# A graph network's edge phase: shifted tables, scans from PSUM, wide casts, and a later scatter

## The reference

```python
def conv(x, W_l, b, W_r):
    agg = segment_sum(x[src], dst, N); deg = segment_sum(1, dst, N)
    return (agg / max(deg, 1)) @ W_l + b + x @ W_r
h = relu(conv(x, W1_l, b1, W1_r))
h = relu(conv(h, W2_l, b2, W2_r))
out = layernorm(x + h @ W3 + b3)      # all float32, biases not zero
```

## Time and profile before

| | |
|---|---|
| median of 3 runs | 3070.76 us (3068.34 to 3070.82) |
| profiled execution | 3069.83 us, span 3068.0 us |
| busy in the span | PE 2858.7, DVE 2459.7, ACT 2066.8, POOL 2239.5 us |
| granted TensorE clock, mean | 0.974 |
| DMA | 488.23 MB, 159 GB/s |

### The profile page before, as it was taken

One profiled execution on the slowest core, in us unless ns is written; L12 is line 12 of the kernel. 1 busy time (PEld: TensorE's weight loads), 2 busy tenths in 40 slices (PEclk: granted clock), 3 DMA queues, 4 the chain that ended last, 5 costly groups with the idle time before them and its releaser, 6 DMA issues. The chain is left out here.

```text
span 3068.0 us, 56367 instructions
## 1 busy us (share of the span) xinstructions
PE 2858.7 (93%) x18433; PEld 2560.7 (83%) x18433; DVE 2459.7 (80%) x4095; ACT 2066.8 (67%) x3188; POOL 2239.5 (73%) x1830
## 2 busy tenths in 40 slices
PE   5999999999999999999999999999998887887885
PEld 4898888888888888888888888888888776777775
DVE  5888888888887878878888788787887876777775
ACT  3777677676766777767767676677776655555554
POOL 5777777777777777777777777777776677777776
PEclk9999999999999999999999999999999898989898
DMA  3444444444444445444444444444443655555553
GB/s 128 147 164 152 156 153 155 150 158 157 157 156 147 161 145 164 151 157 151 155 152 159 156 157 155 146 163 145 164 151 128 211 192 174 193 181 188 194 175 118
DMA packets 253118, 488.23 MB, mean 159 GB/s; under 512 B 37615, under 2 KB 165206, under 8 KB 253090
## 3 DMA queue, kind: packets, MB, share of 16 engines
q1 hardware_dynamic: 202498, 387.58, 37.4%
q0 software_dynamic: 50176, 99.91, 10.8%
q10 hardware_dynamic: 416, 0.40, 0.0%
HBM read 284.67 MB, written 206.22 MB: 160 GB/s over the span
## 5 line engine op out<-in xcount | busy, mean ns | idle before, releaser
L494 ACT ACTIVATE h_full<-pair,bias 128x512 f32<-128x512 f32 x784 | 531.5, 684 | 632.0 <-PE pair L866 616.9
L655 DVE TENSOR_TENSOR h_lo<-h_full,h_hi 128x1024 fp32r<-128x1024 f32 x392 | 658.0, 1679 | 174.7 <-ACT h_hi L496 174.7
L390 POOL TENSOR_TENSOR xb<-xn,b_row 128x1024 f32<-128x1024 f32 x196 | 470.7, 2402 | 225.7 <-DVE y L671 223.8
L344 POOL DMA_INDIRECT xe<-in_x_dram,e_stage x392 | 500.7, 1277 | 177.0 <-issue 97.7
L877 PE MATMUL pair<-w_hi,h_hi 128*128 128x256 f32 x1960 | 553.2, 282 | 30.4 <-DVE h_lo L655 28.7
L877 PE MATMUL pair<-w_hi,h_lo 128*128 128x256 f32 x1960 | 543.0, 277 | 0.0
L877 PE MATMUL pair<-w_lo,h_hi 128*128 128x256 f32 x1960 | 542.5, 277 | 0.0
L856 PE MATMUL pair<-ident,xn 128*128 128x128 f32 x2352 | 336.4, 295 | 128.7 <-DMA xn<-h_tab,c_stage 119.4
L856 PEld LDWEIGHTS pair<-ident,xn 128*128 128x128 f32 x2352 | 301.6, 154 | 163.7 <-issue 115.1
L496 ACT CAST h_hi<-h_full 128x1024 fp32r<-128x1024 f32 x392 | 412.7, 1053 | 12.5
L877 PEld LDWEIGHTS pair<-w_hi,h_hi 128*128 128x128 f32 x1960 | 367.8, 188 | 55.4 <-DVE h_lo L655 51.8
(11 more groups left out here) (117 smaller groups left out, 6583.8 us busy)
## 6 DMA issues: line engine op xcount, KB each, us to landing
xn<-in_x_dram SPq DMA_DIRECT2D x196, 512.0 KB, 3.9
out_dram<-o SPq DMA_DIRECT2D x196, 512.0 KB, 2.7
seg<-seg_tab SPq DMA_DIRECT2D x74, 512.0 KB, 5.0
xdb_tab<-xdb SPq DMA_DIRECT2D x49, 512.0 KB, 4.7
h_tab<-src_h SPq DMA_DIRECT2D x49, 512.0 KB
h_tab<-dst_h SPq DMA_DIRECT2D x49, 512.0 KB, 6.2
xn<-h_tab SPq DMA_DIRECT2D x49, 512.0 KB, 5.2
xb<-xdb_tab SPq DMA_DIRECT2D x49, 512.0 KB, 4.1
```

What stands on the lines that cost most here:

```text
L344: nc.gpsimd.indirect_dma_start(out=xe[:, kind, s], out_offset=None, in_=x, in_offset=bass.IndirectOffsetOnAxis(ap=e_stage[:, kind, s:s + 1 ...
L390: nc.gpsimd.tensor_tensor(xb[:, b], xn[:, u], b3_row[:, :].unsqueeze(1).to_broadcast([P, S, D]), ALU.add).then_inc(xb_ok, 1)
L494: nc.scalar.activation(h_full[:, n, k], ps[:, k], ACT.Relu, bias=bias[:, n, k:k + 1]).then_inc(hf_ok[n], 1)
L655: nc.vector.tensor_tensor(h_lo[:, h], h_full[:, n], h_hi[:, h].bitcast(f32), ALU.subtract).then_inc(hlo_ok[n], 1)
```

## The change

The tables now hold max(z, -b1) instead of z+b1. Since relu(z+b1) = max(z,-b1)+b1, and the segment mean of a constant over a destination's sources is the constant, the readers use the shifted value and b1 moves into the second layer's bias: b2 + W2_r'b1 + W2_l'b1. PE computes the two products once, between the stages (24 matmuls of two columns), from `b1_hi` and `b1_lo`, which DVE makes at the start; DVE adds b2 (`bias_c`). With no relu left to take, the scans read `pair[0]` in PSUM directly, ACT's relu into `h_full` is gone, and `xe_hi`, `xe_lo`, `h_hi`, `h_lo` are each made by one 1024-wide instruction. DVE's step begins with the residual of j-2 and takes its statistics between the means and `mean_low`; ACT's step finishes tile j-3 ahead of `second`, and takes the deviation of j-2 at its end; POOL's step scatters tile j-4. PE's transpose into `pair[0]` waits for the scans of the tile before. The end of the phase drains one tile more.

```diff
             def step(j, b, left):                                   # POOL
                 if left > 1:
                     fetch(j + 2, b)
-                if not (isinstance(j, int) and j < 3):
-                    scatter(j - 3, 1 - b)
+                if not (isinstance(j, int) and j < 4):
+                    scatter(j - 4, b)
                 if not left:
...
+                    for n in range(j - 3, j + 1):
+                        scatter(n, n % 2)
...
-            def front(j, b):                                        # ACT
...
+            def dst_high(j, b):
+                act.wait_ge(c_hd_ps, (j + 1) * K)
+                nc.scalar.copy(xe_hi[:, b], pair[1][:, :, :]).then_inc(c_hdhi_ok, 1)
...
+            def second(j, k):
+                after(act, c_hlo_ok, j)
                 act.wait_ge(c_l2_ps, j * K + k + 1)
+                nc.scalar.activation(h_full[:, 1, k], pair[2][:, k], ACT.Relu, bias=bias_c[:, k:k + 1]).then_inc(c_hf_ok, 1)
+            def second_high(j, b):
+                act.wait_ge(c_hf_ok, (j + 1) * K)
+                nc.scalar.copy(h_hi[:, b], h_full[:, 1]).then_inc(c_hhi_ok, 1)
...
             def step(j, b, left):
                 if left:
-                    front(j + 1, 1 - b)
-                if not (isinstance(j, int) and j < 2):
-                    deviation_edges(j - 2, b)
-                second(j, b, 0)
-                if left:
-                    mean_high(j + 1, 1 - b)
-                second(j, b, 1)
+                    dst_high(j + 1, 1 - b)
                 if isinstance(j, int) and j == 0:
                     for n in range(2):
                         act.wait_ge(y_out[n], 16 * (NG // 2))
+                if not (isinstance(j, int) and j < 3):
+                    finish_edges(j - 3, 1 - b)
+                second(j, 0)
+                if left:
+                    mean_high(j + 1, 1 - b)
+                second(j, 1)
+                second_high(j, b)
                 if not (isinstance(j, int) and j < 2):
+                    deviation_edges(j - 2, b)
+                if not left:
                     finish_edges(j - 2, b)
...
             low_h(0, 0, 0)                                          # DVE, start
+            dve.wait_ge(b_in, 96)
+            nc.vector.tensor_scalar(b1_row[:, :], b1_row[:, :], -1.0, None, ALU.mult).then_inc(b1_ok, 1)
+            nc.vector.tensor_copy(b1_hi[:, :, :], bias[:, 0].unsqueeze(2).to_broadcast([P, K, 2])).then_inc(b1_ok, 1)
+            dve.wait_ge(b1_ok, 2)
+            nc.vector.tensor_tensor(b1_lo[:, :, :], ..., b1_hi[:, :, :].bitcast(f32), ALU.subtract).then_inc(b1_ok, 1)
...
-                                            b1_row[:, :].unsqueeze(1).to_broadcast([P, S, D]), ALU.add).then_inc(src_ok, 1)
+                                            b1_row[:, :].unsqueeze(1).to_broadcast([P, S, D]), ALU.max).then_inc(src_ok, 1)
...
+            def scan(j, b):                                         # DVE, edge phase
+                dve.wait_ge(c_seg_in[b], slot_use(j, b))
+                for k in range(K):
+                    dve.wait_ge(c_hs_ps, j * K + k + 1)
+                    dve.wait_ge(c_run_ok, j * K + k + 1)
+                    nc.vector.tensor_tensor_scan(run[:, k], seg_of(b)[:, 0:G], pair[0][:, k], run[:, k, G - 1:G], ALU.mult, ALU.add)\
+                        .then_inc(c_run_ok, 1)
...
+            def low_dst(j, b):
+                dve.wait_ge(c_hdhi_ok, j + 1)
+                nc.vector.tensor_tensor(xe_lo[:, b], pair[1][:, :, :], xe_hi[:, b].bitcast(f32), ALU.subtract).then_inc(c_hdlo_ok, 1)
...
+            def low_second(j, b):
+                dve.wait_ge(c_hhi_ok, j + 1)
+                nc.vector.tensor_tensor(h_lo[:, b], h_full[:, 1], h_hi[:, b].bitcast(f32), ALU.subtract).then_inc(c_hlo_ok, 1)
...
             def step(j, b, left):
                 early = isinstance(j, int) and j < 2
                 if not early:
+                    residual_edges(j - 2, b)
+                if not (isinstance(j, int) and j < 3):
+                    factors_edges(j - 3, 1 - b)
                 if left:
+                    scan(j + 1, 1 - b)
+                    low_dst(j + 1, 1 - b)
+                    means(j + 1, 1 - b)
                 if not early:
+                    sums(j - 2, b, c_y_ok, c_stats_ok)
                 if left:
                     mean_low(j + 1, 1 - b)
+                if not early:
+                    averages_edges(j - 2, b)
+                low_second(j, b)
...
+            pe.wait_ge(y_ok, NG - 1)                                # PE, between the stages
+            pe.wait_ge(b1_ok, 3)
+            for m in range(K):
+                first = True
+                for w in (X2R, X2L):
+                    for k in range(K):
+                        for wx, a in ((w_hi, b1_hi), (w_lo, b1_hi), (w_hi, b1_lo)):
+                            ins = nc.tensor.matmul(pair[2][:, 0, 2 * m:2 * m + 2], wx[:, w, k, m * P:(m + 1) * P], a[:, k],
+                                                   start=first, stop=w == X2L and k == K - 1 and a is b1_lo)
+                            first = False
...
             def turn_edges(j, b):
                 pe.wait_ge(c_hs_in[b], slot_use(j, b, 16 * S))
-                after(pe, c_hs_ok, j * K)
+                pe.wait_ge(c_run_ok, (j + 1) * K)
```

More of the change, by code:

```diff
@@ L811, in factors_edges @@
                 factors(j, b, c_sd_ok, c_rs_ok, c_nb_ok)
-            for k in range(K):
-                scan(0, 0, k)
+            scan(0, 0)
+            low_dst(0, 0)
             means(0, 0)
-            for k in range(K):
-                low_dst(0, 0, k)
+            dve.wait_ge(bias_ps, 1)
+            nc.vector.tensor_tensor(bias_c[:, :], pair[2][:, 0, 0:2 * K].rearrange("p (k a) -> p k a", a=2)[:, :, 0], bias[:, 1],
+                                    ALU.add).then_inc(bias_ok, 1)
             mean_low(0, 0)
+            dve.wait_ge(o_ok, NG)
             def step(j, b, left):
@@ L822, in step @@
                 if not early:
-                    dve.wait_ge(c_stats_ok, j - 1)
+                    residual_edges(j - 2, b)
+                if not (isinstance(j, int) and j < 3):
+                    factors_edges(j - 3, 1 - b)
                 if left:
-                    scan(j + 1, 1 - b, 0)
+                    scan(j + 1, 1 - b)
+                    low_dst(j + 1, 1 - b)
+                    means(j + 1, 1 - b)
                 if not early:
[L827 to L834, removed]
-                    factors_edges(j - 2, b)
+                    sums(j - 2, b, c_y_ok, c_stats_ok)
                 if left:
                     mean_low(j + 1, 1 - b)
-                low_second(j, b, 1)
-                if isinstance(j, int) and j == 0:
-                    dve.wait_ge(o_ok, NG)
-                else:
-                    residual_edges(j - 1, 1 - b)
-                if not left:
-                    averages_edges(j - 1, 1 - b)
-                    factors_edges(j - 1, 1 - b)
-                    residual_edges(j, b)
-                    averages_edges(j, b)
-                    factors_edges(j, b)
+                if not early:
+                    averages_edges(j - 2, b)
+                low_second(j, b)
+                if not left:
+                    factors_edges(j - 2, b)
+                    for n, c in ((j - 1, 1 - b), (j, b)):
+                        residual_edges(n, c)
+                        sums(n, c, c_y_ok, c_stats_ok)
+                        averages_edges(n, c)
+                        factors_edges(n, c)
             edge_passes(dve, step)
```

54 lines of the change are left out of this document (16 added, 38 removed).

## The result

The changed kernel took 3079.2 us (median of 7 runs, 3074.89 to 3083.91) against 3069.92 for the kernel before (7 runs on the same chip, 3067.49 to 3073.29): a ratio of 1.003, 95% interval 1.0018 to 1.0042. It is slower by 0.3%; 3042 had been forecast. Its profiled execution took 3074.89 for a span of 3073.1.

The account below looks back on a forecast made before the run. POOL, issuing eight indirect DMAs and two small copies a step, was taken to bound the edge phase. Steps -25.6, head -7.0, tail +3.8 and start +0.6 summed to -28.2: median 3042 from 3070.76, own range 3021 to 3055, whole range 3008 to 3063.

Parts of the forecast that it names:

- The change does its work in the second: Of two stages, row tiles up to about 2380 and then the edge phase, the edge phase was to hold the gain.
- Rival B: Edge phase: the two buffers of `o` and the scatter's landing become the loop, step 14.3, 3084; chance 0.11.
- the step: One edge tile's round on POOL, between fetch ends: 13.91 to 13.3 over 42 steps, -25.6.
- The bare time of 12.0: Edge phase: a step with no POOL issue or copy stretched by DVE; stretching is the time beyond it, 1.9 before.
- the squares: Edge phase: stretching of POOL goes with summed squares of DVE hold lengths, 7.16 to 4.47; stretching 1.2, step 13.2.
- a placement: Edge phase: DVE holds laid by hand against POOL's issues; stretching 1.55 with landing at F+9, F a fetch's end, 0.9 at F+11.
- Residual first, wide casts: Edge phase: the new DVE order and 1024-wide operations stay off POOL's path; DVE's 10.5 a step loses some 0.3.
- ACT's order is the risk: Edge phase: ACT's `second` stands behind the wait for the scatter's landing; PE's `mean_low` was still to be in time.
- Head and tail: Ends of the edge phase, scatter four behind: -7.0 until the end of fetch 6, +3.8 after fetch 48.
- Hidden, by 3 only: Edge phase tail: `o` of tile 48 ends 34.5 after the last fetch, its scatter's first issue comes at 37.8.
- A: Edge phase: the three DVE holds fall between POOL's issues, stretching 0.5, step 12.5, 3008; chance 0.2.
- C: Edge phase: stretching only moves or comes from any busy DVE, so only head and tail count, 3068; chance 0.09.

Follow-up runs that it names:

- e1: The changed kernel with its three small new tensors declared last, nothing else differing; 3029.74, ratio 0.9878 to the kernel before.
- e2: The kernel before with an unused tensor of 96 bytes a partition behind `b3_row`; 3118.95, ratio 1.0164 to the kernel before.
- e4: e1 with ACT copying `pair[0]` into `h_full` in SBUF and the scans reading that copy; 3066.83, ratio 0.9989 to the kernel before.
- e5: The kernel before with only tables, bias and PSUM scans changed; old order, 512-wide operations, scatter three behind, small tensors last; 3034.83, ratio 0.9879.
- e7: e1 with the second layer's result left in `pair[2]`, so that `h_lo` reads PSUM; 3025.01, ratio 0.9847 to the kernel before.
- e8: e7 with the scans also working in place in `pair[0]`, from which `mean` reads; 3005.55, ratio 0.9788 to the kernel before.
- e6: e1 with POOL's scatter three steps behind in place of four; 3041.93, ratio 0.9913 to the kernel before.
- e10: e8 with POOL's scatter three steps behind in place of four; 3009.3, ratio 0.9808 to the kernel before.
- e16: The kernel before with 256 unused bytes behind `b3_row`; ratio 0.9996 to the kernel before.

## Why the prediction was wrong, point by point

**The step that failed** is the sum itself: it has no term for the row stage. The prediction put it as "The change does its work in the second", and of the part that touches the row stage, "Adding against taking the maximum with bias is one operation for another: 0". The operation does cost nothing there. The three new tensors cost +48.6: e1 takes it away by moving them, e2 brings it into the kernel before with an unused pad. Of the rivals none names the row stage either, and the range had no room for a loss there. Rival B's 3084 lies near the measured 3079.2 by chance: its mechanism, a longer step through the slots of `o`, is absent. Had the term been in the sum at its measured size, the forecast would have been 3042+49=3091. The edge phase then gave 15 more than forecast (-43.5 against -28.2), and the median lies 4 above the profiled execution.

**The mis-sized term** is the step: -25.6 forecast, -38.0 measured. The bare time of 12.0 and the cause were right, as e4 shows. The stretching was 1.03, where the squares gave 1.2 and I took 1.3 between them and a placement. Taking the estimate from squares alone, 13.2, would have given -30. Of the 1.9 before, 0.5 was the fetch's copy, 709 against 225 after; the squares shrank it in proportion with the rest, and the change took off nearly all of it. The squares are no reliable rule: they gave 1.8, 1.06, 0.7 and 0.35 for e4, e5, e7 and e8, where 1.99, 1.27, 0.96 and 0.43 came, each time too little.

**Residual first, wide casts.** Costed at nothing on the path: right within what the times can tell, by e5 beside e1. ACT's long wait for the landing came as placed, and "ACT's order is the risk" did not come true: POOL waited 4.1 for `o` in 540 us.

**Head and tail.** Head -9.9 for -7.0, tail +4.35 for +3.8: right in sign and mechanism, and no nearer than the spread of heads and tails allows to say. "Hidden, by 3 only" was reckoned for `o` of tile 48 and came true; not reckoned were tiles 45 and 46. Timeline of POOL in e1's tail, first issues of scatters 45, 46 and 48:

```profile
2993.98 0.99 POOL L444 DMA_INDIRECT out_dram<-o,c_stage  x1 [2.11 <-ACT o L579]
...
3001.52 0.99 POOL L444 DMA_INDIRECT out_dram<-o,c_stage  x1 [2.25 <-ACT o L579]
...
3013.56 0.98 POOL L444 DMA_INDIRECT out_dram<-o,c_stage  x1 [0.97 <-POOL c_stage L439]
```

The first two wait some 1.1 and 1.3 beyond the bare 0.97 there. In the kernel after only scatter 45 does (2.10).

**The rivals.** A (12.5 a step, stretching 0.5) did not occur by luck of phase; e8 reached it by taking inputs away. B fell with the kernel after itself, where POOL waited 4.1 for `o` in 540 us, and again with e6 and e10. C fell with e4: the stretching is tied to SBUF inputs, not to a busy DVE. It had borrowed the inference of the Trainium skill, "SBUF — State Buffer", "Who interferes with whom", that descriptor generation needs only the write interface. For these indirect DMAs it doesn't hold: under a scan differing in one operand the issue takes 0.99 or 1.81. The issue also reads its index columns `c_stage` from SBUF, and whether it is that read or the descriptors that is held, no run here shows. The chances have a slip too: 0.6, 0.2 and a third of 0.09 make 0.83 for faster, not 0.85.

**Still open.** Why a distance of 64 is the fast one is not known. A distance of 224 was not tried, nor was moving `h_hi`, `xe_hi` and `mean_hi` one by one. That PE's two reads are what collides is a guess from the distance rule and not shown by itself.

## What to carry to other kernels

A new SBUF tensor, however small, moves every tensor declared after it: where PE is full, as it is here, declare it last, and compare the spacing of unchanged matmuls before and after. When a change is meant for one stage, read the length of the other stages from one repeated line first; here that separated +48.6 from -43.5. Where POOL's indirect DMAs set the pace, give each DVE operation beside them one PSUM input, and stop when the PSUM tile has become a chain of its own.

## What the runs showed of the hardware

- In this kernel the spacing of the matmuls depends on the distance of their two SBUF operands within a partition. At a granted clock of 1.00 those with 256 columns stand 114 ns apart at a distance of 64 modulo 256 bytes, and 118 to 120 at the six other multiples of 32 that were tried; those with 512 columns 229 at 64 and at 0, and 232 to 234 at the five others. That is 30 to 50 us, 1.0 to 1.6%. The period of 256 rests on one run, e16.
- A DVE instruction with two SBUF inputs holds an indirect DMA's issue on POOL until 0.75 to 0.91 after its own end; with one input in PSUM it doesn't (0 of 90 issues in the kernel after). The scan itself takes the same time from either (2.45 and 2.46 for two).
- ACT's wait for a scatter's landing, up to 8.0 and in nearly every step of the kernel after, cost POOL nothing there.
- PE's granted clock in the edge phase, a mean of stretches at 1.00 and at 0.50 (2.4 and 1.2 GHz), rose from 0.90 to 0.97, while PE's busy share rose from 0.81 to 0.86; what it brought by itself was not measured.
